# Row maxima from the fp16 high halves, two heads side by side on 32 rows each, in the attentions of a two-layer transformer kernel

## The reference

```python
# xa0 (layer 0): 16 heads of dk = 16, queries from layernorm(x), keys and values from the context, with biases
q, k, v = x @ Wq + bq, ctx @ Wk + bk, ctx @ Wv + bv
a = softmax(q @ k.T * dk ** -0.5)        # per head, 2048 x 1601
x = x + (a @ v) @ Wo + bo
# a1 and a2 (layer 1): 16 heads of 32 (512 columns in all), no biases on q, k, v
a = softmax(q @ k.T * D ** -0.5)         # a1: 2048 x 2048, a2: 2048 x 1601
if causal:                               # a1 only: after the softmax, keys later than the query are kept
    a = a * (t > s)
x_out = x + (a @ v) @ li1_w + li1_b
```

## Time and profile before

| | us |
|---|---|
| median of 3 runs | 4659.37 |
| lowest and highest run | 4658.74, 4666.88 |
| span of the profiled execution | 4666.5 |
| TensorE matmuls busy in it (86%) | 4034.3 |
| TensorE weight loads busy (beside matmuls) | 1887.4 |
| VectorE busy (61%) | 2859.9 |
| ScalarE busy (42%) | 1944.0 |
| GpSimd busy (20%) | 912.1 |

### The profile page before, as it was taken

The page is one execution under the profiler, slowest core; times in us unless marked ns, Lnnn a source line. Parts: engine busy times, 40 slices in busy tenths (PEclk is TensorE's granted clock), DMA queues, the critical chain, the costliest instruction groups (busy, mean ns, idle before and its releaser), DMA issues. The chain is left out here.

```text
span 4666.5 us, 65472 instructions
## 1 busy us (share of the span) xinstructions
PE 4034.3 (86%) x23278; PEld 1887.4 (40%) x23278; DVE 2859.9 (61%) x5627; ACT 1944.0 (42%) x3868; POOL 912.1 (20%) x369
## 2 busy tenths in 40 slices
PE   5999999628846999999996679999997669999999
PEld 2334333317732332333224423333333446666665
DVE  4787878371145787867754467777771555555554
ACT  0565656201101565656672325555563422222222
POOL 0000000002211000010104037777785300000000
PEclk7898989757966999999987879999998879999999
DMA  2000000016731000000000010000000110000000
GB/s 64 18 18 12 22 8 8 5 40 206 237 109 39 16 8 21 8 21 8 8 1 23 8 37 12 20 10 18 10 6 5 37 39 20 29 19 29 19 19 18
DMA packets 98523, 146.37 MB, mean 31 GB/s; under 512 B 28563, under 2 KB 84058, under 8 KB 91226
## 3 DMA queue, kind: packets, MB, share of 16 engines
q1 hardware_dynamic: 93658, 137.52, 9.4%
q0 software_dynamic: 4608, 5.57, 0.7%
HBM read 98.64 MB, written 9.18 MB: 23 GB/s over the span
## 5 line engine op out<-in xcount | busy, mean ns | idle before, releaser
L486 DVE TENSOR_REDUCE a_part_max<-a_wb 128x1 f32<-128x512 f32 (+1 forms) x2048 | 1167.9, 626 | 301.2 <-PE a_wb L558 291.9
L438 ACT ACTIVATE a_e<-a_sc 128x512 f32<-128x512 f32 (+1 forms) x1472 | 797.9, 598 | 805.9 <-PE a_sc L589 802.8
L558 PE MATMUL a_wb<-a_ks,a_qs 96*128 96x512 f16 (+1 forms) x2048 | 745.8, 371 | 49.6 <-DMA a_qs<-a_stage 28.0
L403 POOL TENSOR_TENSOR a_part_sum<-a_part_sum,a_e 128x2048 f32<-128x2048 f32 x128 | 581.3, 4541 | 141.2 <-ACT a_e L438 78.2
L438 ACT ACTIVATE xa_e<-xa_sc 128x512 f32<-128x512 f32 (+1 forms) x832 | 440.8, 599 | 366.1 <-PE xa_sc L589 365.6
L589 PE MATMUL a_sc<-a_qs,a_ks 97*128 97x512 f16 (+1 forms) x1472 | 546.3, 384 | 12.7 <-DMA a_qs<-a_neg_max 8.0
L486 DVE TENSOR_REDUCE xa_part_max<-xa_wb 128x1 f32<-128x401 f32 x1024 | 513.7, 567 | 61.8 <-PE xa_wb L558 56.5
L558 PEld LDWEIGHTS a_wb<-a_ks,a_qs 96*128 96x128 f16 x2048 | 199.9, 98 | 657.8 <-DVE a_part_max L486 474.0
L1437 ACT ACTIVATE moe_sg<-moe_gp 128x512 f32<-128x512 f32 (+1 forms) x216 | 128.6, 595 | 609.4 <-PE moe_up L1391 609.4
L1466 DVE TENSOR_TENSOR moe_hf<-moe_sg,moe_up 128x512 f32<-128x512 f32 (+1 forms) x216 | 148.2, 686 | 378.9 <-ACT moe_sg L1437 378.9
L558 PE MATMUL xa_wb<-xa_ks,xa_qs 96*128 96x401 f16 x1024 | 345.9, 350 | 17.1 <-DMA xa_qs<-xa_stage 11.7
(11 more groups left out here) (298 smaller groups left out, 4499.9 us busy)
## 6 DMA issues: line engine op xcount, KB each, us to landing
experts_w_up<-in_we SPq DMA_DIRECT2D x32, 1024.0 KB, 6.5
moe_w<-in_wm SPq DMA_DIRECT2D x18, 1088.0 KB, 5.0
experts_w_down<-in_we SPq DMA_DIRECT2D x32, 512.0 KB
a_qs<-a_stage SPq DMA_DIRECT2D x384, 32.0 KB, 1.9
a_ks<-a_stage SPq DMA_DIRECT2D x336, 32.0 KB, 1.9
xa_qs<-xa_stage SPq DMA_DIRECT2D x192, 32.0 KB, 1.9
experts_aw<-in_aw SPq DMA_DIRECT2D x16, 384.0 KB
xa_ks<-xa_stage SPq DMA_DIRECT2D x144, 32.0 KB, 1.9
```

Source lines behind the costliest of these rows:

```text
L403: pool.tensor_tensor(part_sum[:, :, :], part_sum[:, :, :], e[:, (nkt * n + kt) % ering, :, :], ALU.add).then_inc(part_added, 1)
L438: act.activation(e[:r, m % ering, j, :], sc[(HG * m + j) % NSC][:r, :], ACT.Exp, scale=scale).then_inc(exp_done, 1)
L486: dve.tensor_reduce(part_max[:, j, t, k:k + 1], src[:, :mxw], AX.X, ALU.max).then_inc(unit_taken, 1)
L558: last = pe.matmul(dst[:, :mxw], qs[:STACK, j, n % NQ, P * t:P * t + P], ks[:STACK, g % 2, j, mxs[k]:mxs[k] + mxw], start=True, stop=True)
```

## The change

`attention()` is rewritten; its callers pass the width of a head (16 or 32) in place of the scale.

- **Maxima.** A row maximum is now taken from the product of the high halves alone (`qhi`, `khi`, 32 rows in place of 96). ("pair", n, t, h, c) makes two heads at once: two matmuls on two groups of 32 rows of TensorE, into the two banks of one tile `mx` (two such tiles, four banks). VectorE reduces both in one instruction (2 x 401 or 2 x 512 columns). A round has 32 pairs. The scores still subtract the value that the maximum gave, so the softmax stays the same but for rounding.
- **Scores.** The row of ones and maxima is now the first one. In xa0, where a head has 16 values, a score has 3 x 16 + 1 = 49 rows, and two heads lie side by side in 64-row tiles (`place`, `per` = 2); their two scores are issued one after the other. In a1 and a2 a score keeps its 97 rows.
- **Banks.** The score banks (three in xa0, two in a1 and a2) also take the projections and the turned maxima. What they hold is read by ScalarE: a plain copy `raw` of queries and keys (with the bias), the values, the negated maxima; it also spreads the divisors.
- **GpSimd** makes the high and low halves out of `raw`. In a2 it starts a round's sum with the sum of two tiles, so the fill of `part_sum` and one addition in a round go away. The row of ones is filled ahead of ("turn", 0).
- **Value sums** come in two halves of 256 columns (in diagonal tiles: the part from `e`, then the part from `em`), the weight sums after them.
- **Weights** are loaded for one group at a time, into two buffers in turn. In a1 the values lie in a ring of 20 tiles, and those of the next group are projected in the fourth round of a group, not the third.
- One list `order` now drives all five engines.

The core of the diff:

```diff
+    nv = nkt + 4 if causal else 2 * nkt
     NC = NG * NCH
-    NST = 3
-    NQ = 3
-    NWB = 3 if ones_at is None else 4
-    NSC = 3
-    PASSED_WORK, TILE_WORK = 5, 8
+    NST, NQ, NR = 3, 3, 2
     LEAD = 2
     own_sum = ones_at is None
+    NSC = 2 if own_sum else 3
     NCOPY = 2 if own_sum else 1
     den_at = 0 if own_sum else ones_at
     MOVES = 16 * 3 * HG
-
-
-
-    def maxima(n, spans=range(nmx)):
-        return [("max", n, t, j, i) for i in spans for t in range(TPC) for j in range(HG)]
+    per = 2 if dk == 16 else 1
+    parts = 3 * dk
+
+    def place(j):
+
+
+        return 64 * (j % per), j // per
+
+    def pairs(n, spans=range(nmx)):
+        return [("pair", n, t, h, c) for c in spans for t in range(TPC) for h in range(HG // 2)]
 
...
+    order = [("k", 0, 0), ("q", 0), ("k", 0, 1)]
+    for c in range(nmx):
+        order += pairs(0, [c]) + ([("k", 0, c + 2)] if c + 2 < len(kch) else [])
+        if c == 1:
+            order += [("v", 0, b) for b in range(nvb)] + [("q", 1)]
+    order.append(("turn", 0))
...
-            work += maxima(n + 1) + [("turn", n + 1)]
+            work += pairs(n + 1) + [("turn", n + 1)]
         if n + 2 < NC:
-            work.insert(16, ("q", n + 2))
+            work.insert(8, ("q", n + 2))
...
+        for half in range(2):
+            if n < NC:
+                order.append(("s", n, kt, 2 * half))
+                if per == 2:
+                    order.append(("s", n, kt, 2 * half + 1))
+            order += some_work(3 * half)
+            if n < NC and per == 1:
+                order.append(("s", n, kt, 2 * half + 1))
+            order += some_work(3 * half + 1)
+            if m and not passed((m - 1) // nkt, (m - 1) % nkt):
+                order.append(("pv", (m - 1) // nkt, (m - 1) % nkt, half))
+            order += some_work(3 * half + 2)
+        if m and own_sum and not passed((m - 1) // nkt, (m - 1) % nkt) and not on_pool((m - 1) % nkt):
+            order.append(("sum", (m - 1) // nkt, (m - 1) % nkt))
+        if 0 < n < NC and kt == 0:
+            order.append(("out", n - 1))
+    order += [("divisors", NC - 2), ("divide", NC - 2), ("out", NC - 1), ("divisors", NC - 1), ("divide", NC - 1)]
...
-        wb = [ps(f"wb{i}", [P, CH]) for i in range(NWB)]
+        mx = [ps(f"mx{i}", [P, 2, CH]) for i in range(2)]
         sc = [ps(f"sc{i}", [P, CH]) for i in range(NSC)]
         po = ps("po", [P, CH])
...
-            sp.dma_start(wvs[:, :, :, :], wv.rearrange("g p k n -> p g k n")).then_inc(w_loaded["v"], 16)
+            def weights(g):
+                if g >= 2:
+
+                    sp.wait_ge(s_taken, s_at[("q", NCH * (g - 1) - 1)] + 1)
+                for u, src, dst in (("k", wk, wks), ("q", wq, wqs), ("v", wv, wvs)):
+                    sp.dma_start(dst[:, g % 2, :, :], src[g]).then_inc(w_loaded[u][g % 2], 16)
+
+            weights(0)
+            weights(1)
...
+                    for s in range(3):
+                        for j in range(HG):
+                            b, c = place(j)
+                            sp.dma_start(target[b + 1 + dk * s:b + 1 + dk * s + dk, c, :],
+                                         kinds[s][SLOT * j:SLOT * j + dk, :]).then_inc(stacked[i % NST], 16)
...
+        @block.gpsimd
+        def _(pool):
+            def constants():
+                pool.wait_ge(split_ready, sum(order.index(u) < order.index(("turn", 0)) for u in staged))
+                for i in range(per):
+                    pool.memset(ks[64 * i:64 * i + 1, :, :, :], 1.0).then_inc(ones_set, 1)
+                    pool.wait_ge(ones_set, i + 1)
...
+                    pool.wait_ge(s_taken, s_at[u] + 1)
...
+                    pool.tensor_copy(high, raw[:, i % NR, :w]).then_inc(high_ready, 1)
+                    pool.wait_ge(high_ready, i + 1)
+                    pool.tensor_tensor(low[:, i % NST, :w], raw[:, i % NR, :w], high, ALU.subtract).then_inc(split_ready, 1)
...
+                        act.activation(e[:, m % ering, j, :], src[:, :], ACT.Exp, scale=scale,
+                                       accum_out=span_sum[:, n % 2, t, j, c:c + 1]).then_inc(s_taken, 1)
+                    else:
+                        act.activation(e[:r, m % ering, j, :], src[:r, :], ACT.Exp, scale=scale).then_inc(s_taken, 1)
...
+                    if bias is None:
+                        act.activation(raw[:, i % NR, :w], src[:, :w], ACT.Copy).then_inc(s_taken, 1)
+                    else:
+                        act.activation(raw[:, i % NR, :w], src[:, :w], ACT.Identity, bias=bias[:, g:g + 1]).then_inc(s_taken, 1)
...
-                        last = dve.tensor_copy(v[:, g % 2, whole[0]:whole[-1] + 1, :], src[:, :len(whole), :])
+                        at = (nkt * g + whole[0]) % nv
+                        last = act.activation(v[:, at:at + len(whole), :], src[:, :len(whole), :], ACT.Copy)
...
+                    act.activation(neg_max[:, :], src[:HG * TPC, :P], ACT.Copy, scale=-1.0).then_inc(s_taken, 1)
...
+                if u[0] == "pair":
+                    n, t, h, c = u[1:]
+                    dve.tensor_reduce(part_max[:, 2 * h:2 * h + 2, t, c], src[:, :, :mxw], AX.X, ALU.max).then_inc(m_taken, 1)
...
+            def score(u):
+                n, kt, j = u[1:]
+                g, r = n // NCH, kt_rows[kt]
+                dst, (b, c) = tile_of("s", u), place(j)
+                rows = slice(b, b + parts + 1)
...
+                    pe.matmul(dst[:, :], qs[rows, c, n % NQ, P * t:P * t + P],
+                              ks[rows, g % 2, c, CH * span:CH * span + CH], start=True, stop=True).then_inc(s_ready, 1)
                 else:
-                    pe.wait_ge(rowmax_ready, u[1] + 1)
...
+                    pe.matmul(dst[:r, :], ks[rows, g % 2, c, P * kt:P * kt + r], qs[rows, c, n % NQ, :],
+                              start=True, stop=True).then_inc(s_ready, 1)
...
+                n, t, h, c = u[1:]
+                g, dst = n // NCH, tile_of("m", u)
+                if (t, h) == (0, 0):
+                    need = [staged[("q", n)]]
+                    if n % NCH == 0:
+                        need += [staged[("k", g, k)] for k, (o, w) in enumerate(kch) if o < mxs[c] + mxw]
+                    pe.wait_ge(high_ready, max(need) + 1)
+                for i in range(2):
+                    rows = slice(SLOT * (2 * h + i), SLOT * (2 * h + i) + SLOT)
+                    last = pe.matmul(dst[:, i, :mxw], qhi[rows, n % NQ, P * t:P * t + P], khi[rows, g % 2, mxs[c]:mxs[c] + mxw],
+                                     start=True, stop=True)
+                last.then_inc(m_ready, 1)
...
-                        pe.matmul(po[h:h + SLOT, :P * i], w, e[:r, m % ering, j, :P * i], start=False, stop=False)
-                    pe.matmul(po[h:h + SLOT, P * i:P * i + P], w, em[:r, kt % 2, j, :], start=(i == 0), stop=stop)
-                if not own_sum or kt in shared[n]:
+                    w = v[:r, (nkt * g + kt) % nv, h:h + SLOT]
+                    if diag is None:
+                        o = CH // 2 * half
+                        last = pe.matmul(po[h:h + SLOT, o:o + CH // 2], w, e[:r, m % ering, j, o:o + CH // 2],
+                                         start=(kt == first and half == 0), stop=(stop and half == 1))
+                    elif half:
+                        last = pe.matmul(po[h:h + SLOT, P * diag:P * diag + P], w, em[:r, kt % 2, j, :], start=(diag == 0), stop=stop)
+                    elif diag:
+                        pe.matmul(po[h:h + SLOT, :P * diag], w, e[:r, m % ering, j, :P * diag], start=False, stop=False)
...
```

508 lines of the change are left out of this document (251 added, 257 removed).

## The result

The changed kernel takes **4749.45 us** (median of 4 runs, 4745.95 to 4755.98), the kernel before 4662.85 us (4 runs, 4658.74 to 4666.88). The ratio is 1.0191, with a 95% interval from 1.0177 to 1.0206: slower by 87 us. The forecast was 4750 us. Executions more than 1.5% longer than the fastest of their kernel were in a slower state and are left out of the ratios; this concerns two of the four of `pairs_serial`.

The account below looks back on a forecast made before the run. TensorE was taken to set the pace of the 48 rounds. Its net -35, waits +60 and starts -54 gave -29 us; the clock's +120 made +91 on the 4659.4 us median: 4750, range 4585 to 4890.

Parts of the forecast that it names:

- Streams saved: TensorE in the rounds: maxima in pairs and xa0's scores side by side save one stream each, together 360 us.
- Changes of shape at 0.10 us: TensorE in the rounds: 2625 more changes of the array's tile shape at 0.10 us each cost 262 us.
- Rival 2: Changes between groups of rows cost less than those of columns: about 4590 us, or 4470 without the clock's loss; chance 0.08.
- rival 3: Pairs do not run side by side, or fp16 weights of 32-row tiles load slowly: 5000 to 5100 us; chance 0.05.
- Weights and halves: TensorE in the rounds: unhidden first weights of each pair cost 37 us, value sums cut in two halves 26 us.
- Waits, 60 us: New waits for ScalarE, VectorE and score banks in the rounds cost 60 us, bounds nothing and 140.
- Rival 4: Two score banks starve ScalarE; called unlikely alone and counted inside the 60 us of waits, no chance of its own.
- The starts, -54: Ahead of each attention's rounds: maxima no longer wait for the DMAs, 18 us saved at each of three starts.
- The clock: TensorE's clock falls in more of xa0's rounds and a few of a1: 5 slow round-equivalents, +120 us.

Follow-up runs that it names:

- pairs_serial: Changed kernel with each pair as two query chunks of one head on the same 32 rows, one after the other: 5198.3 and 5230.06 us, 1.119 of before.
- values_whole: Changed kernel with the value sums of a key tile in one piece of 512 columns, diagonal tiles still in two: 4850.34 us, ratio 1.0402.
- a1_before: Changed kernel with the causal attention a1 alone taken back to the function of before: 4642.34 us, ratio 0.9977.
- scores_twice: Changed kernel with each score of a passed tile in a1 issued twice into the same bank, 384 extra products: 4746.77 us, ratio 1.0191.
- before_two_banks: Kernel before, with two score banks in place of three in a1 and a2, the freed bank given to the maxima: 4686.39 us, ratio 1.0057.
- spread_early: Changed kernel with the spread of the divisors as its own list entry, three units behind divisors and four ahead of divide: 4675.22 us, ratio 1.0021.
- pairs_together: Changed kernel with both pairs of the same 128 queries next to each other in the list, four heads on four row groups: 4786.04 us, ratio 1.0254.
- bias_first: Changed kernel with xa0's one-row products for the bias of the values made one product ahead of each bank: 4727.44 us, ratio 1.0131.

## Why the prediction was right, and where it was not

**Streams saved: right.** The products of a pair stand 2 to 5 ns apart, a pair and its change take 0.27 us for 401 columns and 0.32 for 512, two scores 0.32; `pairs_serial` gives the stream back, 0.17 us a pair.

**Changes of shape at 0.10 us: right**, for columns and for rows. Each change, from 49 to 32 rows, from 97 to 32, from 32 to 128 by 32 and back, adds 0.10 us to the stream. At the slow clock it is 0.11 (see the last section). Rival 2 (changes between groups of rows for less) and rival 3 (no work side by side) are out.

**Weights and halves: right as a cost, wrong as a sum.** The halves were put at +26 us and a part of the changes, 0.05 + 0.10 us each, and 0.15 was measured. `values_whole` shows that without them the kernel is 101 us slower. The step that failed is "each half pays the start and the stagger again" as if nothing came back for it; what the halves do for ScalarE's supply was left out.

**Waits, 60 us: the size right, the content not.** TensorE's waits in the rounds are 23.5, 43.9 and 25.3 us before, and 46.1, 67.4 and 36.3 after: 57 more. The largest single one, the spread of the divisors, was in no term; I had counted ScalarE's work for it and not its place in ScalarE's queue. With what hung on it, it was worth 74 us. Rival 4, two score banks, was called unlikely alone; in the kernel before they cost 22 us.

**The starts, -54: right**, -64 measured, in the way described: the waits for the stacked copies are gone. The prediction's 96 us for xa0's start take in the first 11 us of its rounds, which changes nothing in this term.

**The clock: right that it decides, wrong on the place.** I put +120 us on it, all in xa0. xa0 has 0.91 (0.95 before) and not the 0.7 to 0.85 that I named, and its rounds are 16 us shorter; a1 has 0.83 and is 123 us longer. The step that failed reads "I expect the clock to fall where it fell, to stay down until well into the round after, and to fall in other rounds of xa0 and a few of a1 (passed tiles)". I weighed the share of narrow products in a tile of xa0. I did not weigh that in a passed tile of a1 there are no value sums at all, that ScalarE sets the pace there, so that what TensorE saves becomes idle time. I had even written that down for the waits ("what TensorE saves there is lost") and not drawn the consequence for the clock. That the 120 us reserved for xa0 and the 123 us that a1 lost are nearly one number is chance. The size of the term doesn't hold either. An estimate from the windows: if TensorE set the pace everywhere, a slow stretch would cost half its length, which adds up to the length of the rounds times (1 - clock). That was some 36 us in xa0 and 19 in a1 before, and is 64, 184 and 17 in xa0, a1 and a2 now: up to 210 us more, not 120, and all but some 30 of that outside xa0. ScalarE's pace in the passed tiles makes the true loss smaller, by how much no run shows. By this estimate the rest of the sum was as much too high as the clock term was too low. The 4750 that fits to a microsecond is luck and no proof of the reasoning.

**What is shown and what not.** Shown: the loss is a1's (`a1_before`); it goes with the clock, and more scores over 97 rows in the passed tiles bring the clock back (`scores_twice`); two banks alone don't do it (`before_two_banks`); some 30% of it goes with the wait for the spread (`spread_early`).

That the idle time is the cause is argued, not shown. For it speaks the kernel before: in a1's last round, which has passed tiles and no maxima, TensorE waited for ScalarE between its scores, and the clock fell at 2426.4 us. The 8 us ahead of that hold scores over 97 rows, one group of value sums and one of weight sums, and no product over 32 rows:

```profile
2418.40:2426.40 8.00, 5.90 (x29) 1.21 (x27) 0.00 (x0) 7.63 (x25) 0.00 (x0) 1.00 0.00 0
2426.40:2457.10 30.70, 29.28 (x79) 5.74 (x79) 0.00 (x0) 26.47 (x85) 2.53 (x2) 0.50 0.00 1
```

Against it as the whole cause speak `pairs_serial`, where the clock fell after 8 us without a gap, and `pairs_together`, where a1 has more idle time and the same clock. In the passed tiles of the change both stand together, gaps and products over 32 rows, and no run takes one away and leaves the other. Not tried either: the pairs in a1 with three score banks, for which no bank of the eight is free. So how the loss divides between gaps, narrow products and banks stays open.

## What to carry to other kernels

Where another engine sets the pace, work taken from TensorE turns into gaps; here such stretches, with narrower products in them, lost the clock and cost more than was saved. Before making products narrower or fewer, look for the stretches in which TensorE already waits. If all engines follow one list, an entry that makes one of them wait for another's result wants an entry of its own for that result, some steps ahead; moving the waiting entry alone does nothing. And a forecast should be checked by its parts, stage by stage: here the total was right to 1 us, with its clock term, 120 us, in the wrong attention.

## What the runs showed of the hardware

- Four products over 32 rows each on four groups of rows take 0.28 us with their change of shape, as long as two.
- A change of shape costs nearly the same at either clock. At 2.4 GHz a pair of 512 columns takes 0.32 us to the next score and a stream 0.22. At 1.2 GHz (the changed kernel, 1699.58 to 1701.63) a pair takes 0.54 to the next score, one score with the change behind it 0.54 too and two scores 0.97, so a stream takes 0.43 and the change 0.11.
- A busy TensorE is not enough for the full clock. In `pairs_serial`, where each product of the maxima had the array to itself with 32 of its rows, the clock fell at 447.9 us after 8 us in which TensorE was busy throughout; xa0's rounds had 0.76 there and 0.91 in the change.
- The loss of the clock is partly a matter of chance. xa0's third round took 45.8 us in the change and 62.8 in `scores_twice`, its eleventh 45.9 and 59.5 in `bias_first`, each with the same code; only work before or after them differed.
